# GpSimd adds the two halves of the products itself, in place of an accumulating transfer

## The chip, the cores and the metric

One Trainium2 chip, one of its cores. The metric is the device time of one execution, in microseconds (us). The engines are TensorE (PE; its weight loads are PEld), VectorE (DVE), ScalarE (ACT), GpSimd (POOL) and SyncE (SP, which here only issues transfers).

## What is computed

A recommendation tower over a batch of 1024: 39 embeddings of 16 numbers each are gathered, two layers of a compressed interaction network follow, and an MLP ends it.

```python
def cin_layer(x0, xk, W, b):                      # x0: (1024, 39, 16)
    out = jnp.einsum('bhd,bmd,shm->bsd', xk, x0, W) + b[None, :, None]
    return jax.nn.relu(out)

e = stack([tbl_f[ids[:, f]] for f in range(39)], axis=1)
x1 = cin_layer(e, e, W1, b1)                      # (1024, 128, 16)
x2 = cin_layer(e, x1, W2, b2)                     # (1024, 128, 16)
z = concatenate([x1.sum(-1), x2.sum(-1)], axis=-1)
h = concatenate([z, dense_ctx], axis=1)
h = maximum(h @ W_top1 + b_top1, 0)
h = maximum(h @ W_top2 + b_top2, 0)
y = h @ W_top3
```

The change touches only the second layer: for each batch row and each of the 16 embedding columns d, the sum over the 39 features m of `x0[b, m, d]` times a row of 128 numbers that TensorE has made from `x1` and `W2[:, :, m]`.

## The kernel before

The batch is cut into 8 **tiles** of 128 rows, and the 16 embedding columns of a tile into 4 **chunks** of 4. A chunk is 512 columns wide for the first layer. In the second layer each of its 4 embedding columns is a **column tile**, `ct` in the code, with the 128 batch rows on the partitions: 128 column tiles in all, 16 a batch tile.

*TensorE* (L526 on) works off one list. For each chunk it goes through 40 banks of PSUM, 10 a column tile; a bank has the products with four features (512 numbers), the tenth with three, and takes three matmuls each (L564; `w2h` and `w2l` are a weight split into two parts, `x1h` and `x1l` the same for the first layer's result). Five banks form a ring. Between the banks of one chunk stand the seven matmuls of the first layer for the next chunk (L548, at the places `CONTRACT_AT`), and, at bank 28, four transposes that lift the chunk after it from `emb_rep` into the PSUM tile `e_rep` (L537, called the lift here). In chunks 17 and 29 the matmuls of the MLP's two batches are put in too.

*ScalarE and VectorE* share the banks of a column tile. ScalarE takes banks 0, 2, 4, 6 and 8: for each of its 20 features it multiplies 128 numbers by the embedding's value and writes them to `prod` (L363), five banks of 512 in a row. `prod` has three buffers (`P_RING`). VectorE takes the other banks and adds its 19 features into `acc` as it scales them (L468, L470). Later VectorE merges both, once a chunk for the chunk before: L479 adds the two accumulators, L483 adds GpSimd's sum `a_sum`, L490 applies the ReLU and adds to `p2acc`. They stand at banks 22, 27 and 29 (`MERGE_AT`). L431 multiplies `e_rep` by the shifted copies of the embeddings, `z`, for the first layer.

*GpSimd* gathers the embeddings (L255, one indirect transfer for each of the 39 features of a tile) and adds up the 20 products of each column tile, 2560 numbers a row, to 128:

1. L266 (`add_by_transfer`): a transfer adds the upper half of `prod`, 1280 numbers, to the lower half, once ScalarE has written the column tile;
2. L284 (`add_quarters`): 640 + 640 into `tree`;
3. L291 (`add_inner`): 256 + 256;
4. L296 (`add_pair`): 128 + 128;
5. L305 (`add_last`): the 128 left over is added, and the result goes to `a_sum`.

These five steps of different column tiles are staggered: in the step for `ct`, GpSimd issues the transfer of `ct`, then the adds of `ct - 1` and `ct - 2`. Before them come two or three gathers for a later tile, until all are issued (`gathers_before`: all gathers of tile t stand ahead of column tile 16t - 7). The last column tile has its first step as a GpSimd add, L272 (`add_first`).

Three waits tie this together. ScalarE starts a column tile only when L284 has read the buffer of `prod` it will write (`sum3`). SyncE copies a tile's gathered embeddings to `emb_rep` (L207) when all 39 gathers have landed, and TensorE's first lift of that tile waits for the copy; it is in the place of column tile 16t - 6. VectorE's merge L483 waits for `a_sum`. SyncE also stores each lifted chunk (L216) and loads the shifted copies `z` (L224, nine transfers a chunk).

Of the kernel before, what the change touches and what calls it, by code (L numbers as in the profile page):

```python
# [9 lines left out]
ALU = mybir.AluOpType  # L10
# [5 lines left out]
S = 128  # L16
# [6 lines left out]
CTS = CHUNKS * DC  # L23
# [11 lines left out]
NA, NV = len(A_BANKS), len(V_BANKS)  # L35
# [39 lines left out]
def build(nc, dram, tables, out):  # L75
    with ExitStack() as ctx:
# [6 lines left out]
        def sem(name):  # L83
            return ctx.enter_context(nc.semaphore(name))
# [64 lines left out]
        p1_done = sem("p1_done")  # L149

        bank_ready, a_free, v_step = sem("bank_ready"), sem("a_free"), sem("v_step")
        in_sum = [sem(f"in_sum{r}") for r in range(2)]
        sum3, sum2, sum1, sum0 = sem("sum3"), sem("sum2"), sem("sum1"), sem("sum0")
        sum_first = sem("sum_first")
        merge_step, p2_done = sem("merge_step"), sem("p2_done")
# [3 lines left out]
        def wait(eng, s, value):  # L159
            if value > 0:  # L160
                eng.wait_ge(s, value)
# [3 lines left out]
        def gathers_before(ct):  # L165
            return min((TILES - 1) * M, -(-M * (ct + 7) // 16))

        def v_steps(ct, i):
            return ct * VM + V_BEFORE[i]
# [72 lines left out]
        @block.gpsimd  # L242
        def _(pool):
            def gather(n):
                tile, f = divmod(n, M)
                if f == 0 and tile == 0:
                    pool.wait_ge(in_idx0, 16)
                if f == 0 and tile == 1:
                    pool.wait_ge(in_idx, 16)
                if f == 0 and tile >= E_SLOTS:  # L250
                    last = (tile - E_SLOTS + 1) * CPT * DC
                    pool.wait_ge(v_step, v_steps(last, 0))
                    pool.wait_ge(a_free, last * NA)
                    pool.wait_ge(lifted, (tile - E_SLOTS + 1) * CPT)
                nc.gpsimd.indirect_dma_start(  # L255
                    out=emb[:, tile % E_SLOTS, f * D:(f + 1) * D], out_offset=None, in_=tables[f],
                    in_offset=bass.IndirectOffsetOnAxis(ap=idx[:, tile, f:f + 1], axis=0),
                ).then_inc(in_emb[tile % E_SLOTS], 16)

            def products(ct):  # L260
                return prod[:, ct % P_RING, :, :].rearrange("p a n -> p (a n)")

            def add_by_transfer(ct):
                pool.wait_ge(a_free, (ct + 1) * NA)
                half = 2 * NA * S
                nc.gpsimd.dma_start(products(ct)[:, 0:half], products(ct)[:, half:2 * half], accum_op=ALU.add  # L266
                                    ).then_inc(in_sum[ct % 2], 16)

            def add_first(ct):
                half = 2 * NA * S  # L270
                pool.wait_ge(a_free, (ct + 1) * NA)
                nc.gpsimd.tensor_tensor(products(ct)[:, 0:half], products(ct)[:, 0:half], products(ct)[:, half:2 * half],  # L272
                                        ALU.add).then_inc(sum_first, 1)

            def add_quarters(ct):
                n = NA * S
                if ct < CTS - 1:
                    pool.wait_ge(in_sum[ct % 2], 16 * (ct // 2 + 1))
                else:
                    pool.wait_ge(sum_first, 1)  # L280
                wait(pool, sum0, ct - 1)
                if ct == 0:
                    pool.wait_ge(w1_summed, 1)
                nc.gpsimd.tensor_tensor(tree[:, ct % 2, 0:n], products(ct)[:, 0:n], products(ct)[:, n:2 * n], ALU.add  # L284
                                        ).then_inc(sum3, 1)

            def add_inner(ct):
                pool.wait_ge(sum3, ct + 1)
                t = tree[:, ct % 2, :]
                n = NA // 2 * S  # L290
                nc.gpsimd.tensor_tensor(t[:, 0:n], t[:, 0:n], t[:, n:2 * n], ALU.add).then_inc(sum2, 1)  # L291

            def add_pair(ct):
                pool.wait_ge(sum2, ct + 1)
                t = tree[:, ct % 2, :]
                nc.gpsimd.tensor_tensor(t[:, 0:S], t[:, 0:S], t[:, S:2 * S], ALU.add).then_inc(sum1, 1)  # L296

            def add_last(ct):
                pool.wait_ge(sum1, ct + 1)
                c, j = divmod(ct, DC)  # L300
                if j == 0:
                    wait(pool, merge_step, 3 * (c - 1))
                t = tree[:, ct % 2, :]
                last = (NA - 1) * S if NA % 2 else 2 * S
                nc.gpsimd.tensor_tensor(a_sum[:, c % 2, j, :], t[:, 0:S], t[:, last:last + S], ALU.add).then_inc(sum0, 1)  # L305

            for n in range(M):
                gather(n)
            begun = M
            for ct in range(CTS):  # L310
                for n in range(begun, M + gathers_before(ct)):
                    gather(n)
                begun = max(begun, M + gathers_before(ct))
                if ct < CTS - 1:
                    add_by_transfer(ct)
                if ct:
                    add_quarters(ct - 1)
                if ct > 1:
                    add_pair(ct - 2)
                if ct:  # L320
                    add_inner(ct - 1)
                if ct > 1:
                    add_last(ct - 2)
            add_pair(CTS - 2)
            add_last(CTS - 2)
            add_first(CTS - 1)
            add_quarters(CTS - 1)
            add_inner(CTS - 1)
            add_pair(CTS - 1)
            add_last(CTS - 1)  # L330

# [344 lines left out]
```

## Time and profile before

| | |
|---|---|
| median of 3 runs | 1255.2 us (1251.39 to 1255.94) |
| the profiled execution | 1253.83 us |
| its span, first to last instruction | 1252.0 us |
| mean granted clock of TensorE | 0.989 of full |
| busy: PE, DVE, ACT, POOL | 92%, 74%, 64%, 68% of the span |
| GpSimd's adds of 640, 256, 128, 128 (L284, L291, L296, L305) | 239.3, 136.7, 111.3, 89.1 us |
| the transfer issues L266, the gathers L255 | 127 of 975 ns, 312 of 990 ns |
| software queue (gathers, accumulating transfers) | 85.81 MB, 36.9% of the 16 DMA engines' span |
| hardware queue (SyncE's transfers) | 67.92 MB, 22.0% |

"Busy" is the time in which an engine had an instruction under way. Records of one engine overlap: an add that is dispatched behind a transfer issue begins in the record before the issue ends. How long one operation holds the engine is better read from start to start, or from end to end, of neighbours with no wait between them. The span is one execution's; the median is over three.

### The profile page before, as it was taken

To read this page: it belongs to the slowest core of one execution; us is meant where nothing else is said; L and a number is where in the kernel's file an instruction comes from. 1 tells how busy PE (TensorE), PEld (TensorE's weight loads), DVE (VectorE), ACT (ScalarE), POOL (GpSimd) and SP (SyncE) were. 2 spreads that over 40 slices of the span, in tenths; PEclk is the share of its full clock that TensorE was granted. 3 is DMA by queue.
4 is the path that set the end of the run, shared out by engine and by line. 5 is a ranking of instruction groups with operands and counts; after the bars stand their busy time and mean duration, and the time that the engine had idled before them with its cause. 6 is when DMAs were issued, how large, how long until landed. Compare 5 with 4: busy or idle time off the path is not lost.

```text
span 1252.0 us, 17389 instructions
## 1 busy us (share of the span) xinstructions
PE 1155.7 (92%) x4556; PEld 849.7 (68%) x4556; DVE 928.8 (74%) x2846; ACT 796.9 (64%) x2702; POOL 848.6 (68%) x956
## 2 busy tenths in 40 slices
PE   0069999999999999999999999999999999999996
PEld 0037777777777777777776567777777776776775
DVE  2028878887878878788887468888887888774786
ACT  3026766667667766667666466777666666664683
POOL 7725777877787777787786467777777773442455
PEclk9989999999999999999999999999999999999997
DMA  5145666666765666677666267666665676642541
GB/s 163 41 103 106 125 148 130 142 129 134 172 123 119 123 151 125 128 142 151 145 140 121 44 138 156 136 119 124 144 125 124 137 158 133 139 100 62 119 92 35
DMA packets 66346, 154.85 MB, mean 124 GB/s; under 512 B 13219, under 2 KB 18981, under 8 KB 66246
## 3 DMA queue, kind: packets, MB, share of 16 engines
q0 software_dynamic: 28272, 85.81, 36.9%
q1 hardware_dynamic: 37974, 67.92, 22.0%
q8 instruction: 36, 0.59, 0.2%
q14 instruction: 64, 0.52, 0.2%
HBM read 58.59 MB, written 4.20 MB: 50 GB/s over the span
## 4 chain that ended last, share of the span: by engine, by line
POOL 43%; DMA 23%; issue 20%; PE 10%; another core or an unknown queue 2%; ACT 1%; SPq 1%; DVE 0%; POOLq 0%; ACTq 0%; DVEq 0%
DMA prod<-prod 19%; POOL emb L255 15%; POOL tree L284 11%; PE bank L564 7%; POOL tree L291 5%; POOL prod L266 5%; POOL tree L296 3%; POOL a_sum L305 3%; PE l_acc L548 2%; DMA z<-e_shifted 2%; DMA emb_rep<-emb 1%; DMA e_shifted<-e_t 1%; SPq L224 1%; ACT prod L363 0%
## 5 line engine op out<-in xcount | busy, mean ns | idle before, releaser
L363 ACT ACTIVATE prod<-bank,emb 128x128 f32<-128x128 f32 x2560 | 728.6, 372 | 368.8 <-PE bank L564 346.8
L470 DVE SCALAR_TENSOR_TENSOR acc<-bank,emb,acc 128x128 f32<-128x128 f32 x2176 | 613.3, 345 | 138.8 <-PE bank L564 118.4
L564 PE MATMUL bank<-w2h,x1h 128*128 128x512 f32 (+1 forms) x1280 | 537.0, 420 | 5.7 <-DVE x1l L436 4.5
L564 PE MATMUL bank<-w2l,x1h 128*128 128x512 f32 (+1 forms) x1280 | 499.7, 390 | 0.0
L564 PE MATMUL bank<-w2h,x1l 128*128 128x512 f32 (+1 forms) x1280 | 473.6, 433 | 0.0
L255 POOL DMA_INDIRECT emb<-tbl,idx x312 | 309.0, 990 | 82.0 <-issue 77.8
L564 PEld LDWEIGHTS bank<-w2h,x1h 128*128 128x128 f32 x1280 | 242.3, 189 | 119.2 <-issue 54.0
L564 PEld LDWEIGHTS bank<-w2h,x1l 128*128 128x128 f32 x1280 | 241.1, 188 | 87.5 <-issue 35.1
L266 POOL DMA_DIRECT2D prod<-prod x127 | 123.9, 975 | 243.7 <-ACT prod L363 239.7
L284 POOL TENSOR_TENSOR tree<-prod 128x640 f32<-128x640 f32 x128 | 239.3, 1870 | 66.5 <-DMA prod<-prod 66.4
L564 PEld LDWEIGHTS bank<-w2l,x1h 128*128 128x128 f32 x1280 | 241.8, 189 | 60.1 <-issue 17.5
L548 PE MATMUL l_acc<-z,w 117*128 117x512 f32 (+1 forms) x448 | 233.5, 604 | 16.1 <-DVE z L431 12.6
L431 DVE TENSOR_TENSOR z<-e_rep,z 117x512 f32<-117x512 f32 (+1 forms) x224 | 152.9, 684 | 121.0 <-DMA z<-e_shifted 80.3
L291 POOL TENSOR_TENSOR tree<-tree 128x256 f32<-128x256 f32 x128 | 136.7, 1068 | 0.2
L548 PEld LDWEIGHTS l_acc<-z,w 117*128 117x128 f32 (+1 forms) x448 | 84.3, 192 | 43.5 <-DVE z L431 16.7
L296 POOL TENSOR_TENSOR tree<-tree 128x128 f32<-128x128 f32 x128 | 111.3, 870 | 0.1
L305 POOL TENSOR_TENSOR a_sum<-tree 128x128 f32<-128x128 f32 x128 | 89.1, 696 | 0.2
L537 PE MATMUL e_rep<-ident_f,emb_rep 128*117 128x128 f32 x128 | 29.3, 352 | 63.6 <-DMA emb_rep<-emb 63.6
L537 PEld LDWEIGHTS e_rep<-ident_f,emb_rep 128*117 128x117 f32 x128 | 29.0, 287 | 67.7 <-issue 57.9
L470 DVE SCALAR_TENSOR_TENSOR acc<-bank,emb,b_row 128x128 f32<-128x128 f32 x128 | 44.8, 350 | 27.1 <-PE bank L564 25.0
L468 DVE TENSOR_SCALAR acc<-bank,emb 128x128 f32<-128x128 f32 x128 | 44.1, 344 | 0.0
L347 ACT COPY e_t<-e_rep 117x512 f32<-117x512 f32 x32 | 19.5, 611 | 34.7 <-PE e_rep L537 33.8
(75 smaller groups left out, 299.7 us busy)
## 6 DMA issues: line engine op xcount, KB each, us to landing
prod<-prod POOLq DMA_DIRECT2D x127, 640.0 KB
z<-e_shifted SPq DMA_DIRECT2D x160, 234.0 KB
emb_rep<-emb SPq DMA_DIRECT2D x8, 936.0 KB
z<-e_shifted SPq DMA_DIRECT2D x96, 78.0 KB
emb<-tbl,idx POOLq DMA_INDIRECT x312
z<-e_shifted SPq DMA_DIRECT2D x32, 156.0 KB
e_shifted<-e_t SPq DMA_DIRECT2D x32, 128.0 KB, 2.8
prod<-w_by_h SPq DMA_DIRECT2D x3, 832.0 KB
```

The costliest lines, as they stand in the source:

```text
L255: nc.gpsimd.indirect_dma_start(out=emb[:, tile % E_SLOTS, f * D:(f + 1) * D], out_offset=None, in_=tables[f], in_offset=bass.IndirectOffse ...
L266: nc.gpsimd.dma_start(products(ct)[:, 0:half], products(ct)[:, half:2 * half], accum_op=ALU.add).then_inc(in_sum[ct % 2], 16)
L284: nc.gpsimd.tensor_tensor(tree[:, ct % 2, 0:n], products(ct)[:, 0:n], products(ct)[:, n:2 * n], ALU.add).then_inc(sum3, 1)
L291: nc.gpsimd.tensor_tensor(t[:, 0:n], t[:, 0:n], t[:, n:2 * n], ALU.add).then_inc(sum2, 1)
L296: nc.gpsimd.tensor_tensor(t[:, 0:S], t[:, 0:S], t[:, S:2 * S], ALU.add).then_inc(sum1, 1)
L305: nc.gpsimd.tensor_tensor(a_sum[:, c % 2, j, :], t[:, 0:S], t[:, last:last + S], ALU.add).then_inc(sum0, 1)
L363: last = nc.scalar.activation(prod[:, ct % P_RING, i, n * S:(n + 1) * S], bank[:, (ct * NB + k) % RING, n * S:(n + 1) * S], ACT.Copy, scal ...
L431: nc.vector.tensor_tensor(z[0:rows, f % 2, t, :], e_rep[0:rows, :], z[0:rows, f % 2, t, :], ALU.mult).then_inc(f_made, 1)
L470: nc.vector.scalar_tensor_tensor(dst, src, scale, dst if step else b2_row[:, :], ALU.mult, ALU.add).then_inc(v_step, 1)
L537: last = nc.tensor.transpose(e_rep[0:KP * M, d * P:(d + 1) * P], by_d[:, q * DC + d, :], ident_f[:, :])
L548: nc.tensor.matmul(l1_acc[:, :], w1[0:rows, t, :], z[0:rows, f % 2, t, :], start=(t == 0), stop=(t == NF - 1)).then_inc(f_used, 1)
L564: last = nc.tensor.matmul(out_bank[:, 0:b - a], x, w[:, a:b], start=(n == 0), stop=(n == 2))
```

## The change

The transfer is gone. Each column tile has its 1280-element add on GpSimd (`add_first`, L265 of the new kernel), so `in_sum`, the semaphores of the transfers, go too, and `sum_first` counts the column tiles. The stagger becomes shorter: in the step for `ct` GpSimd does the first three adds of `ct` and, put between them, the last two of `ct - 1`.

```diff
@@ add_by_transfer, removed
-            def add_by_transfer(ct):
-                pool.wait_ge(a_free, (ct + 1) * NA)
-                half = 2 * NA * S
-                nc.gpsimd.dma_start(products(ct)[:, 0:half], products(ct)[:, half:2 * half], accum_op=ALU.add
-                                    ).then_inc(in_sum[ct % 2], 16)
-
             def add_first(ct):
                 half = 2 * NA * S
                 pool.wait_ge(a_free, (ct + 1) * NA)
@@ add_quarters
-                if ct < CTS - 1:
-                    pool.wait_ge(in_sum[ct % 2], 16 * (ct // 2 + 1))
-                else:
-                    pool.wait_ge(sum_first, 1)
+                pool.wait_ge(sum_first, ct + 1)
                 wait(pool, sum0, ct - 1)
@@ the loop over the column tiles, behind the gathers
-                if ct < CTS - 1:
-                    add_by_transfer(ct)
-                if ct:
-                    add_quarters(ct - 1)
-                if ct > 1:
-                    add_pair(ct - 2)
-                if ct:
-                    add_inner(ct - 1)
-                if ct > 1:
-                    add_last(ct - 2)
-            add_pair(CTS - 2)
-            add_last(CTS - 2)
-            add_first(CTS - 1)
-            add_quarters(CTS - 1)
-            add_inner(CTS - 1)
+                if ct == CTS - 1:
+                    add_pair(ct - 1)
+                    add_last(ct - 1)
+                add_first(ct)
+                if 0 < ct < CTS - 1:
+                    add_pair(ct - 1)
+                add_quarters(ct)
+                if 0 < ct < CTS - 1:
+                    add_last(ct - 1)
+                add_inner(ct)
             add_pair(CTS - 1)
             add_last(CTS - 1)
```

GpSimd's list in the stretch where gathers still run, one step with three gathers, before:

```order
L255 DMA emb<-tbl,idx 128x16 x3
L266 DMA prod<-prod 128x1280
L284 TENSOR_TENSOR tree<-prod 128x640
L296 TENSOR_TENSOR tree<-tree 128x128
L291 TENSOR_TENSOR tree<-tree 128x256
L305 TENSOR_TENSOR a_sum<-tree 128x128
L255 DMA emb<-tbl,idx 128x16 x2
```

And the same place in the changed kernel, whose lines are numbered anew:

```order
L254 DMA emb<-tbl,idx 128x16 x3
L265 TENSOR_TENSOR prod<-prod 128x1280
L286 TENSOR_TENSOR tree<-tree 128x128
L274 TENSOR_TENSOR tree<-prod 128x640
L295 TENSOR_TENSOR a_sum<-tree 128x128
L281 TENSOR_TENSOR tree<-tree 128x256
L254 DMA emb<-tbl,idx 128x16 x2
```

The wide add stands where the issue stood. The 640- and 256-element adds are now those of the column tile just written, the 128-element adds those of the one before it.

The end of GpSimd's list before, from the last transfer issue on:

```order
L266 DMA prod<-prod 128x1280
L284 TENSOR_TENSOR tree<-prod 128x640
L296 TENSOR_TENSOR tree<-tree 128x128
L291 TENSOR_TENSOR tree<-tree 128x256
L305 TENSOR_TENSOR a_sum<-tree 128x128
L284 TENSOR_TENSOR tree<-prod 128x640
L296 TENSOR_TENSOR tree<-tree 128x128
L291 TENSOR_TENSOR tree<-tree 128x256
L305 TENSOR_TENSOR a_sum<-tree 128x128
L296 TENSOR_TENSOR tree<-tree 128x128
L305 TENSOR_TENSOR a_sum<-tree 128x128
L272 TENSOR_TENSOR prod<-prod 128x1280
```

And in the changed kernel, from the wide add of the last column tile but one:

```order
L265 TENSOR_TENSOR prod<-prod 128x1280
L286 TENSOR_TENSOR tree<-tree 128x128
L274 TENSOR_TENSOR tree<-prod 128x640
L295 TENSOR_TENSOR a_sum<-tree 128x128
L281 TENSOR_TENSOR tree<-tree 128x256
L286 TENSOR_TENSOR tree<-tree 128x128
L295 TENSOR_TENSOR a_sum<-tree 128x128
L265 TENSOR_TENSOR prod<-prod 128x1280
```

Ahead of the last wide add there were the four adds behind the last transfer and two short ones; now there are the two short ones. What follows the last wide add is the same in both.

## Rows read from the trace of the kernel before

**Rows 1.** Busy time of each engine, its share of the span, instructions.
```profile
PE 1155.7 (92%) x4556; PEld 849.7 (68%) x4556; DVE 928.8 (74%) x2846; ACT 796.9 (64%) x2702; POOL 848.6 (68%) x956
```

**Rows 2.** PE's timeline, the lifts: start, us, what, [idle before <-releaser].
```profile
181.22 1.06 PE L537 MATMUL e_rep<-ident_f,emb_rep 128*117 128x128 f32 x4 [1.20 <-DMA emb_rep<-emb]
...
528.35 0.87 PE L537 MATMUL e_rep<-ident_f,emb_rep 128*117 128x128 f32 x4
...
562.31 0.87 PE L537 MATMUL e_rep<-ident_f,emb_rep 128*117 128x128 f32 x4
...
596.95 1.06 PE L537 MATMUL e_rep<-ident_f,emb_rep 128*117 128x128 f32 x4 [0.58 <-DMA emb_rep<-emb]
...
757.00 0.87 PE L537 MATMUL e_rep<-ident_f,emb_rep 128*117 128x128 f32 x4
...
1035.96 1.07 PE L537 MATMUL e_rep<-ident_f,emb_rep 128*117 128x128 f32 x4 [2.29 <-DMA emb_rep<-emb]
```

**Rows 3.** Waits from 181.2 to 597 us: total, times, longest.
```profile
POOL prod L266 <- ACT prod L363: 33.5, 15, 3.3
...
POOL tree L284 <- DMA prod<-prod: 32.5, 12, 3.4
DVE z L431 <- DMA z<-e_shifted: 30.9, 13, 3.4
```

**Rows 4.** POOL's timeline, one step with three gathers, one with two.
```profile
531.50 0.97 POOL L266 DMA_DIRECT2D prod<-prod  x1 [3.17 <-ACT prod L363]
...
539.33 1.02 POOL L266 DMA_DIRECT2D prod<-prod  x1
539.96 2.01 POOL L284 TENSOR_TENSOR tree<-prod 128x640 f32<-128x640 f32 x1
541.48 0.90 POOL L296 TENSOR_TENSOR tree<-tree 128x128 f32<-128x128 f32 x1
...
545.93 1.03 POOL L266 DMA_DIRECT2D prod<-prod  x1
```

**Rows 5.** The chain of waits: start, us, what.
```profile
52.96 4.31 DMA emb_rep<-emb
...
307.37 1.57 POOL tree L284
...
314.38 6.61 DMA emb_rep<-emb
```

**Rows 6.** The timeline at the end, POOL, DVE and ACT.
```profile
1224.51 0.68 DVE L483 TENSOR_TENSOR t_sum<-t_sum,a_sum 128x512 f32<-128x512 f32 x1
...
1225.79 1.89 POOL L284 TENSOR_TENSOR tree<-prod 128x640 f32<-128x640 f32 x1
1225.89 2.44 DVE L490 SCALAR_TENSOR_TENSOR p2acc<-t_sum,p2acc 128x512 f32<-128x512 f32 x1
...
1227.32 1.30 POOL L296 TENSOR_TENSOR tree<-tree 128x128 f32<-128x128 f32 x1
...
1231.81 1.14 ACT L363 ACTIVATE prod<-bank,emb 128x128 f32<-128x128 f32 x4 [0.26 <-PE bank L564]
...
1234.66 2.88 POOL L272 TENSOR_TENSOR prod<-prod 128x1280 f32<-128x1280 f32 x1
1234.80 3.15 DVE L483 TENSOR_TENSOR t_sum<-t_sum,a_sum 128x384 f32<-128x384 f32 x1 [0.95 <-POOL a_sum L305]
```

**Rows 7.** Waits from 94 to 175 us.
```profile
POOL prod L266 <- ACT prod L363: 33.9, 4, 20.4
...
POOL tree L284 <- DMA prod<-prod: 5.1, 2, 2.8
```

**Rows 8.** Waits from 1036 us to the end.
```profile
POOL prod L266 <- ACT prod L363: 108.5, 21, 10.9
```

**Rows 9.** Busy time by stretch, and the granted clock (PEclk), behind a lift.
```profile
core 0: us, PE busy (x) PEld busy (x) DVE busy (x) ACT busy (x) POOL busy (x), PEclk, DMA share, GB/s
1036.70:1041.00 4.30, 4.30 (x14) 3.64 (x14) 2.18 (x4) 2.52 (x9) 1.70 (x2) 0.60 0.09 19
```

More of the change, by code:

```diff
@@ L151, in build @@
         bank_ready, a_free, v_step = sem("bank_ready"), sem("a_free"), sem("v_step")
-        in_sum = [sem(f"in_sum{r}") for r in range(2)]
         sum3, sum2, sum1, sum0 = sem("sum3"), sem("sum2"), sem("sum1"), sem("sum0")
```

## The prediction

> **What bounds the kernel now.** I read the engines' busy time first, then TensorE's timeline for its period, then GpSimd's waits, then GpSimd's timeline for one step, and last VectorE beside GpSimd. TensorE is busy 92% of the span [rows 1], so it is the bound before the change. Its period is best read at the transposes that lift a chunk into `e_rep`, once a chunk of four column tiles. The undisturbed distance is 562.31 - 528.35 = 33.96 us [rows 2], so a batch tile (four chunks, 16 column tiles) needs at least 4 x 33.96 = 135.8 us of TensorE. The tiles' first lifts stand at 181.22, 596.95 (three tiles later), 757.00 and 1035.96 (two tiles later) [rows 2]: 138.6 us a tile, then 160.1 us for the tile in which the first MLP batch runs, then 139.5 us. About 3 us a tile are lost to small waits, and the queue of transfers has a hand in them: VectorE waits 30.9 us in three tiles for `z` [rows 3].
>
> The reader has to see next how near GpSimd is behind. In the three tiles from 181.2 to 597 it waits 33.5 us for products and 32.5 us for the accumulating transfer [rows 3], 66.0 in all, so **22.0 us a tile** is all the spare time it has. Then there is a tight loop that an engine table does not show. The last gather of a tile releases the copy into `emb_rep`, which releases the tile's first lift on TensorE; that lift already waits, 0.58 us at 596.95 and 2.29 us at 1035.96 [rows 2]. So GpSimd cannot fall behind without TensorE stopping at the next tile, whatever the three buffers of `prod` allow.
>
> **The change, part by part.**
>
> *The issue goes, the wide add comes.* One step of GpSimd before, with no wait in it: 539.33 - 531.50 = 7.83 us with three gathers, 545.93 - 539.33 = 6.60 us with two [rows 4]. From the start of the issue at 539.33 to the end of the 640-element add (539.96 + 2.01) are 2.64 us [rows 4]; that add without an issue ahead of it takes 1.57 [rows 5]; the issue is worth 1.07 us. The wide add is already in the kernel once, for the last column tile: 2.88 us [rows 6]. Upper bound: twice the 640-element add, 3.14. Lower bound: I have no row below 2.88, and the row is of the same shape, so I take it. Net **+1.81 us a step**. The order of the rest (an add of the column tile before between two dependent adds) keeps each dependent add one instruction apart, as before, so I cost its waits at nothing; if that cover failed, some 0.1 us a step would come on top.
>
> The GPSIMD Engine Reference of the Trainium skill (section 3.1) has 4497 ns for a float32 add of 2048 elements, which makes an estimate of 2.81 us for 1280. By it the forecast would be some 6 us lower; the measured 2.88 decides.
>
> *A tile of 16 steps.* 39 gathers in 16 steps are nine steps with two and seven with three: 9 x (6.60 + 1.81) + 7 x (7.83 + 1.81) = 143.2 us. The other way to it: 16 x 1.81 = 29.0 us are added to an engine that has 22.0 us to spare, so it overruns by 7 us before anything else is counted. At 143.2 us against TensorE's 135.8, **GpSimd becomes the bound** wherever gathers still run.
>
> *The port shared with VectorE.* Three merges a chunk on VectorE read two SBUF operands. The one that began at 1225.89, beside GpSimd's add from 1225.79, took 2.44 us, and the one at 1234.80 took 3.15 us, just until the 2.88 us add had ended and its own work was done [rows 6]; the same work took 0.68 at 1224.51, while GpSimd waited [rows 6]. GpSimd pays too: the 128-element add behind such a merge shows 1.30 us instead of 0.90 [rows 4, 6], about 0.5 us with what follows. So far most merges fall into gathers and waits of GpSimd. Afterwards GpSimd adds for 5.95 us of each 9, two thirds of the time: 12 merges a tile x 2/3 x 0.5 = 4.0 us. VectorE's own delay, up to 2.9 us a merge, costs nothing while GpSimd is the bound, since TensorE then has slack.
>
> The page SBUF — State Buffer of the Trainium skill (section "Who interferes with whom") states this as an exclusive lock for the whole instruction, between a VectorE instruction with two SBUF inputs and a GpSimd instruction that reads SBUF. By that rule the trace agrees (3.15 us behind 2.88), and it is the page's rule that speaks most against this change: where a transfer held no port of the engines, the longest GpSimd add of the step now holds it.
>
> *The loop.* The lift of a new tile comes late by what GpSimd is late, and then GpSimd waits once for the products of that delayed column tile: 0 to 2 us, taken as 1. A tile comes to 143.2 + 4.0 + 1.0 = **148.2 us**.
>
> *What the transfer gives back.* 1280 floats in each of 128 partitions, 640 KB a column tile, leave the queues. The copy to `emb_rep` takes 4.31 us on idle queues at 52.96 and 6.61 us under load at 314.38 [rows 5]; about 2 us once a tile, which only moves the loop's phase and is given to the first tile below. VectorE's waits for `z` shrink, but TensorE gains nothing by it while GpSimd holds the pace.
>
> *The sum, on the profiled span of 1252.0 us.*
> - To the first lift of tile 1: ten steps x 1.81 = 18 us against waits of 33.9 - 20.4 + 5.1 = 18.6 us [rows 7]. The copy is shorter, merges cost a little: +1.
> - Three tiles to 596.95: 3 x (148.2 - 138.6) = +28.8.
> - The tile with the MLP: TensorE needs 160.1, more than GpSimd's 148.2: 0.
> - Two tiles to 1035.96: 2 x (148.2 - 139.5) = +17.4, less 2 because the MLP stretch lets GpSimd catch up: +15.4.
> - After that no gathers are left: GpSimd waits 108.5 us for products there [rows 8], and 22 steps add 40. TensorE is the bound again: 0, as longer waits of VectorE at the port and shorter ones for `z` about cancel.
> - The end: the last wide add started at 1234.66 behind the last transfer's adds; ScalarE's products end at 1231.81 + 1.14 = 1232.95 [rows 6], and now only two short adds may stand between: -1.5.
>
> Together +43.7: span 1295.7, and with the 1.8 us around the span (1253.8 - 1252.0) **1297 us**. The profiled execution lies 1.4 below the median of 1255.2 us, within their scatter, so I leave the number there.
>
> **Rivals.**
> 1. *The port costs GpSimd little* (merges come at fixed places in TensorE's order and may keep falling into gathers, as most did). Tiles of 144.2 us: 5 x 4 = 20 less, 1277 us. Chance 0.17.
> 2. *The stops at each tile cost the clock too.* After the 2.29 us wait the granted clock is 0.60 from 1036.7 to 1041, between the 1.2 and the 2.4 GHz level [rows 9]: 4.3 x 0.4 = 1.7 us. If every lift now waits longer and this comes on top, and the wide add is nearer 3.0 than 2.88, I get 1309 us. Against it: behind the lift GpSimd, not TensorE, is late. Chance 0.13.
> 3. *Faster: the freed queues decide.* If the wide add took at most 2.1 us in the stream (2.88 - 12.4/16), GpSimd would need no more than TensorE's 135.8 a tile, and TensorE would lose its waits for transfers: 3 x 2.8 + 2 x 3.7 + 3 (MLP tile) + 1 + 1.5 = 21 less, 1232 us. For it: 30.9 us of waits for `z` in three tiles. Against it: the one row there is, 2.88. Chance 0.08.
> 4. *Level*: a wide add of about 2.4 us and few collisions, losses and gains cancelling, 1255 us. Chance 0.04.
> The forecast keeps 0.58.
>
> **Numbers.** Without the port, and with an add of 2.75 us instead of 2.88 (5 x 16 x 0.13 = 10 less), I come to 1266; with an add of 3.0 us and the clock to 1309 and some 7 more for an add up to the 3.14 bound on part of the steps; the range 1266 to 1316 leaves out the rivals 3 and 4 (0.12) and some tail. A measurement tells about 0.5% (6 us) from no change. Faster 0.08, same 0.05, slower 0.87.
>
> **What would show it.** Right: GpSimd's waits in the three middle tiles near 0 to 2 us a tile instead of 22; the tiles' first lifts 147 to 149 us apart and TensorE waiting several us at each for `emb_rep`, or for ScalarE, which waits for a buffer of `prod`; GpSimd's queue moving the gathers alone; merges of 1.5 to 3 us; after the last tile's lift the old pace. The wide add at 2.9 us and steps of 8.4 and 9.6 us check the price. Wrong: lifts less than 140 us apart, or GpSimd still waiting 10 us a tile for products.

## The result and the profile after

The changed kernel is **slower**: a median of 1292.9 us over five executions (1292.0 to 1300.7) against 1255.0 us before, a ratio of 1.033 with a 95% interval of 1.031 to 1.036. The forecast was 1297 us, slower. A second set of runs of the same kernel, at the end of the study, gave 1288.9 us (1288.3 to 1289.4), ratio 1.028 (1.024 to 1.032) to the kernel before, which had 1252.8 us in that set.

The profile shown here is of the longest of the first five executions, 1300.7 us with a span of 1298.9; the other four lie between 1292.0 and 1293.5. The last experiment has a second profile, of an execution of 1288.5 us; here they are called the first and the second profile.

First the page: busy time of each engine, and the software queue (packets, MB, share of the 16 DMA engines).

```profile
PE 1170.8 (90%) x4556; PEld 858.4 (66%) x4556; DVE 1005.6 (77%) x2846; ACT 797.7 (61%) x2702; POOL 1089.3 (84%) x956
...
q0 software_dynamic: 9984, 2.58, 2.4%
```

Against [rows 1], TensorE's busy share fell from 92% to 90% and GpSimd's rose from 68% to 84%. The software queue moves 2.58 MB instead of 85.81. TensorE's lifts, as in [rows 2] (start, us, what, idle before and what ended it):

```profile
184.45 1.06 PE L522 MATMUL e_rep<-ident_f,emb_rep 128*117 128x128 f32 x4 [4.23 <-DMA emb_rep<-emb]
...
629.17 1.21 PE L522 MATMUL e_rep<-ident_f,emb_rep 128*117 128x128 f32 x4 [3.75 <-DMA emb_rep<-emb]
...
796.15 0.87 PE L522 MATMUL e_rep<-ident_f,emb_rep 128*117 128x128 f32 x4
...
1087.76 1.21 PE L522 MATMUL e_rep<-ident_f,emb_rep 128*117 128x128 f32 x4 [3.69 <-DMA emb_rep<-emb]
```

Three tiles from 184.45 to 629.17 take 444.7 us, 148.2 each, against 138.6 before. The tile with the MLP takes 167.0 against 160.1, the two after it 291.6 against 279.0 together. Each of the lifts but the one behind the MLP waits 3.7 us or more for the copy, where the waits were 0.58 to 2.29. What waits in those three tiles (total, times, longest), to set beside [rows 3]:

```profile
PE e_rep L522 <- DMA emb_rep<-emb: 11.8, 3, 4.2
PE bank L549 <- DVE acc L455: 10.6, 12, 4.0
POOL prod L265 <- ACT prod L348: 8.1, 2, 4.5
```

GpSimd's 66 us of waits are down to 8.1. VectorE no longer waits for `z` at all in these tiles. But TensorE now waits for the banks that VectorE has to free (L549 is the matmul, L455 VectorE's scaled add): 10.6 us, up to 4.0 at once. GpSimd's step, against [rows 4]:

```profile
446.35 2.97 POOL L265 TENSOR_TENSOR prod<-prod 128x1280 f32<-128x1280 f32 x1
...
455.97 2.95 POOL L265 TENSOR_TENSOR prod<-prod 128x1280 f32<-128x1280 f32 x1
...
464.34 2.95 POOL L265 TENSOR_TENSOR prod<-prod 128x1280 f32<-128x1280 f32 x1
```

9.62 us with three gathers and 8.37 with two, where 9.64 and 8.41 were forecast.

The merges are the new thing (L464, L468 and L475 of the new kernel). The busy time of the instructions on `t_sum` over the length of three tiles, first before, then after; the two stretches begin at different places of the tile, but each holds 36 merges (stretch, its length, VectorE's busy us and count, TensorE's granted clock, DMA share, GB/s):

```profile
225.50:641.10 415.60, 27.91 (x36) 1.00 0.66 136
```

```profile
181.00:626.00 445.00, 63.94 (x36) 0.97 0.25 56
```

36 such instructions take 63.9 us instead of 27.9. The worst of them, in the timeline of the changed kernel:

```profile
483.02 2.97 POOL L265 TENSOR_TENSOR prod<-prod 128x1280 f32<-128x1280 f32 x1
...
483.27 6.26 DVE L475 SCALAR_TENSOR_TENSOR p2acc<-t_sum,p2acc 128x512 f32<-128x512 f32 x1
...
485.94 0.47 POOL L286 TENSOR_TENSOR tree<-tree 128x128 f32<-128x128 f32 x1
...
486.35 1.54 POOL L274 TENSOR_TENSOR tree<-prod 128x640 f32<-128x640 f32 x1
487.84 0.45 POOL L295 TENSOR_TENSOR a_sum<-tree 128x128 f32<-128x128 f32 x1
488.25 0.72 POOL L281 TENSOR_TENSOR tree<-tree 128x256 f32<-128x256 f32 x1
...
490.62 0.80 PE L549 MATMUL bank<-w2h,x1h 128*128 128x512 f32 x1 [3.95 <-DVE acc L455]
...
496.09 2.96 POOL L265 TENSOR_TENSOR prod<-prod 128x1280 f32<-128x1280 f32 x1 [4.49 <-ACT prod L348]
```

The merge began 0.25 us after the wide add and ended at 489.53. Its own work is 0.68 us, so it got its turn at 488.85, when all **five** adds of the step were about done, not when the wide add was. TensorE then stood 3.95 us for VectorE's bank, and GpSimd 4.49 us for the products of the column tile that came late by it.

### The profile page after: what moved, and what is told of

Read it like the earlier page. It is cut to its first block, busy times and chain, and to the rows that moved or that the text cites. A ratio compares the mean times of both kernels' runs of the same rounds, so it can differ in the third digit from the quotient of the medians.

```text
span 1298.9 us, 17389 instructions
## 1 busy us (share of the span) xinstructions
PE 1170.8 (90%) x4556; PEld 858.4 (66%) x4556; DVE 1005.6 (77%) x2846; ACT 797.7 (61%) x2702; POOL 1089.3 (84%) x956
## 3 DMA queue, kind: packets, MB, share of 16 engines
q0 software_dynamic: 9984, 2.58, 2.4%
## 4 chain that ended last, share of the span: by engine, by line
POOL 57%; PE 21%; issue 14%; DVE 2%; DMA 2%; another core or an unknown queue 2%; ACT 1%; SPq 0%; POOLq 0%; DVEq 0%; ACTq 0%
POOL prod L265 22%; PE bank L549 15%; POOL emb L254 13%; POOL tree L274 11%; POOL tree L281 5%; PE l_acc L533 4%; POOL a_sum L295 3%; POOL tree L286 3%; PE misc L568 1%; DVE acc L455 1%; DMA prod<-w_by_h 1%; DVE p2acc L475 1%; PE misc L571 1%; DMA z<-e_shifted 0%
## 5 line engine op out<-in xcount | busy, mean ns | idle before, releaser
L455 DVE SCALAR_TENSOR_TENSOR acc<-bank,emb,acc 128x128 f32<-128x128 f32 x2176 | 612.5, 342 | 177.8 <-PE bank L549 164.2
L549 PE MATMUL bank<-w2h,x1h 128*128 128x512 f32 (+1 forms) x1280 | 553.4, 432 | 24.7 <-DVE acc L455 20.2
L549 PE MATMUL bank<-w2l,x1h 128*128 128x512 f32 (+1 forms) x1280 | 504.3, 394 | 0.0
L265 POOL TENSOR_TENSOR prod<-prod 128x1280 f32<-128x1280 f32 x128 | 380.9, 2975 | 117.5 <-ACT prod L348 115.3
L549 PE MATMUL bank<-w2h,x1l 128*128 128x512 f32 (+1 forms) x1280 | 477.5, 437 | 0.0
L549 PEld LDWEIGHTS bank<-w2h,x1h 128*128 128x128 f32 x1280 | 246.0, 192 | 143.6 <-issue 66.0
L549 PEld LDWEIGHTS bank<-w2h,x1l 128*128 128x128 f32 x1280 | 244.6, 191 | 88.9 <-issue 35.1
L549 PEld LDWEIGHTS bank<-w2l,x1h 128*128 128x128 f32 x1280 | 245.5, 192 | 64.0 <-issue 22.9
L274 POOL TENSOR_TENSOR tree<-prod 128x640 f32<-128x640 f32 x128 | 200.0, 1562 | 0.2
L281 POOL TENSOR_TENSOR tree<-tree 128x256 f32<-128x256 f32 x128 | 94.0, 735 | 0.2
L286 POOL TENSOR_TENSOR tree<-tree 128x128 f32<-128x128 f32 x128 | 69.7, 544 | 0.2
L455 DVE SCALAR_TENSOR_TENSOR acc<-bank,emb,b_row 128x128 f32<-128x128 f32 x128 | 44.5, 347 | 29.4 <-PE bank L549 27.6
L295 POOL TENSOR_TENSOR a_sum<-tree 128x128 f32<-128x128 f32 x128 | 59.0, 461 | 0.2
L468 DVE TENSOR_TENSOR t_sum<-t_sum,a_sum 128x512 f32<-128x512 f32 (+2 forms) x33 | 57.1, 1730 | 0.5 <-POOL a_sum L295 0.5
L464 DVE TENSOR_TENSOR t_sum<-acc 128x512 f32<-128x512 f32 (+2 forms) x33 | 49.3, 1493 | 0.0
```

Source lines behind the costliest of these rows:

```text
L455: nc.vector.scalar_tensor_tensor(dst, src, scale, dst if step else b2_row[:, :], ALU.mult, ALU.add).then_inc(v_step, 1)
L549: last = nc.tensor.matmul(out_bank[:, 0:b - a], x, w[:, a:b], start=(n == 0), stop=(n == 2))
```

## The experiments

All but e4, e8, e10 and e12 are edits of the changed kernel; those four are edits of the kernel before.

**e1: two of three merges read one SBUF operand.** The merge sum goes to the PSUM tile `misc` wherever the MLP does not use it.

```diff
+                in_psum = c + 1 not in BATCH_IN and c < CHUNKS - 1
+                merged = misc[:, :].rearrange("p (j s) -> p j s", j=DC) if in_psum else t_sum
+                if n == 0 and in_psum and c in BATCH_IN:
+                    dve.wait_ge(mlp_act, MLP_STEPS * (BATCH_IN.index(c) + 1))
...
-                    nc.vector.tensor_tensor(t_sum[:, a:b, :], t_sum[:, a:b, :], a_sum[:, c % 2, a:b, :], ALU.add
+                    nc.vector.tensor_tensor(merged[:, a:b, :], merged[:, a:b, :], a_sum[:, c % 2, a:b, :], ALU.add
...
```

The first and the third merge have `merged` in place of `t_sum` too.

> The changed kernel with VectorE's merge sum t_sum in the PSUM tile misc (except in the two MLP chunks and the last one), so that two of the three merges of a chunk read one SBUF operand. Port theory: the merges of 2 to 6 us at the second and third place go back to 0.7 us, TensorE's stop of about 4 us behind each tile's first lift and GpSimd's wait of 4.5 us that follows it go, and GpSimd loses fewer half microseconds to VectorE: 1270 to 1282 us against 1293. Rival, GpSimd's own adds alone set the time and VectorE's waits lie beside them: 1290 to 1296.

Measured: 1273.5 us (1273.2 to 1274.9), ratio to the kernel before 1.015 (1.010 to 1.021); 19.4 less than the first set of the changed kernel and 15.4 less than the second. The second merge, where its sum is in PSUM (line, count, busy us, mean ns):

```profile
L472 DVE TENSOR_TENSOR misc<-misc,a_sum 128x512 f32<-128x512 f32 x29 | 20.0, 688 | 0.0
```

None of these 29 takes more than 0.69 us, nor does any third merge that reads `misc`. The first merge still reads two SBUF operands, and 6 of the 12 in three tiles still take over 1 us. Its lifts:

```profile
328.31 1.21 PE L526 MATMUL e_rep<-ident_f,emb_rep 128*117 128x128 f32 x4 [6.17 <-DMA emb_rep<-emb]
...
615.99 1.21 PE L526 MATMUL e_rep<-ident_f,emb_rep 128*117 128x128 f32 x4 [6.32 <-DMA emb_rep<-emb]
```

Two tiles of 143.8 us. The rival that VectorE's waits lie beside the path falls. In these tiles and the one ahead of them GpSimd stands idle for only 0.5 us before its wide adds, so 143.8 us a tile is close to its bare list of adds and gathers (143.2 forecast), and most of what lay above it came from the merges that now read one SBUF operand.

**e2: all gathers four column tiles earlier.**

```diff
-            return min((TILES - 1) * M, -(-M * (ct + 7) // 16))
+            return min((TILES - 1) * M, -(-M * (ct + 11) // 16))
```

> The changed kernel with every gather issued four column tiles earlier. Loop theory: the waits for emb_rep at the tiles' first lifts (3.8 us each) vanish, GpSimd no longer waits for products behind a lift, and the MLP tile loses its extra 7 us in part, but 143 us of work a tile remain: 1270 to 1284 us, GpSimd's wait for products near zero between 181 us and the last gather. Rival, throughput alone: GpSimd's list is as long as before, 1289 to 1296. A third: the late gathers are the whole loss, and the time falls to 1255 or below.

Measured: 1293.7 us (1293.1 to 1294.2), in the range of the rival. The lifts:

```profile
121.47 0.87 PE L522 MATMUL e_rep<-ident_f,emb_rep 128*117 128x128 f32 x4
...
333.77 0.87 PE L522 MATMUL e_rep<-ident_f,emb_rep 128*117 128x128 f32 x4
...
481.23 0.87 PE L522 MATMUL e_rep<-ident_f,emb_rep 128*117 128x128 f32 x4
...
628.72 0.87 PE L522 MATMUL e_rep<-ident_f,emb_rep 128*117 128x128 f32 x4
```

No lift waits any more, and these two tiles still take 147.5 us each; the one ahead of them takes 144.4 and the one behind the MLP 138.5. GpSimd never waits for products in the three tiles, but 35 of their 36 merges now take over 1 us, where the changed kernel has 15 of 36 in either profile. So 147.5 us is GpSimd's list with a collision at nearly every merge, and what the early gathers may have given, the collisions took. Why the merges now fall beside adds is not shown. Part of the result is something else: the third lift stands at 121.47 instead of 111.88, because three engines stood still at the start (ScalarE for 7.1 us, VectorE for 9.4):

```profile
92.11 0.58 ACT L332 COPY e_t<-e_rep 117x512 f32<-117x512 f32 x1 [7.11 <-remote]
...
95.65 3.20 ACT L348 ACTIVATE prod<-bank,emb 128x128 f32<-128x128 f32 x12 [2.95 <-remote]
95.70 0.35 DVE L455 SCALAR_TENSOR_TENSOR acc<-bank,emb,b_row 128x128 f32<-128x128 f32 x1 [9.38 <-remote]
```

What they waited for is in no record; it came with the longer run of gathers before the first column tile, in e12 and e13 too, and stays open.

**e3: a wide add of half the width**, 640 elements. It leaves out the other half of that add.

```diff
-                nc.gpsimd.tensor_tensor(products(ct)[:, 0:half], products(ct)[:, 0:half], products(ct)[:, half:2 * half],
+                nc.gpsimd.tensor_tensor(products(ct)[:, 0:640], products(ct)[:, 0:640], products(ct)[:, half:half + 640],
```

> The changed kernel with a wide add of 640 elements instead of 1280; it leaves out half of that add. If GpSimd's adds set the pace, a step is 1.4 us shorter, a tile needs some 125 us of GpSimd, TensorE is the bound again, and as the queues are free of the transfers it runs at nearly 136 us a tile: 1226 to 1240 us, below the kernel before. If something else in the change costs (the order of the adds, buffers that come free later), 1255 or more.

Measured: 1225.2 us (1224.2 to 1227.9).

```profile
315.56 0.87 PE L522 MATMUL e_rep<-ident_f,emb_rep 128*117 128x128 f32 x4
...
587.20 0.87 PE L522 MATMUL e_rep<-ident_f,emb_rep 128*117 128x128 f32 x4
```

Two tiles in 271.6 us, 135.8 each: TensorE's undisturbed period to the tenth, with none of the 3 us a tile lost before. So the change is worth 30 us of the 1255 where GpSimd can keep up, and its order and its buffers show no cost. How much of the 30 is the free queues' and how much the shorter stagger's, no run separates.

**e9: a wide add of 1024 elements**, the same edit with 1024, which leaves out a fifth of the add.

> The changed kernel with a wide add of 1024 elements; it leaves out a fifth of that add. By the rows 1280 elements take 2.96 us and 640 take 1.6, so a step is 0.55 us shorter and a tile 8.8: 139 us of GpSimd with the port's collisions, still a little over TensorE's 135.8: 1240 to 1256 us. Rival, GpSimd stops being the bound only at a much narrower add: over 1265.

Measured: 1238.8 us (1236.8 to 1240.4), a little under the range. The add (line, busy us, mean ns) and the effect:

```profile
L265 POOL TENSOR_TENSOR prod<-prod 128x1024 f32<-128x1024 f32 x128 | 310.6, 2426 | 120.4 <-ACT prod L348 117.7 <-issue 1.1
```

0.55 us less a step, and tiles of 137 to 139 us. Of the 54 us that e9 saves against the first set (50 against the second), 5 tiles x 16 x 0.55 = 44 are the shorter add: what the last 256 elements cost GpSimd is seen in the time. The rest is not assigned.

**e5: the wide adds in the order of the kernel before.**

```diff
...
                 add_first(ct)
-                if 0 < ct < CTS - 1:
-                    add_pair(ct - 1)
-                add_quarters(ct)
-                if 0 < ct < CTS - 1:
-                    add_last(ct - 1)
-                add_inner(ct)
+                if ct:
+                    add_quarters(ct - 1)
+                if ct > 1:
+                    add_pair(ct - 2)
+                if ct:
+                    add_inner(ct - 1)
+                if ct > 1:
+                    add_last(ct - 2)
...
```

> The changed kernel's wide adds in the order of the kernel before (the wide add where the transfer was issued, then the shorter adds of the two column tiles before it). Theory: the work decides, not the stagger: 1288 to 1300 us against 1293. Rival, the shorter stagger itself costs or gains: under 1285, or over 1303 because the buffers of prod come free one step later.

Measured: 1298.4 us (1297.7 to 1313.2), ratio to the kernel before 1.039 (1.032 to 1.046), which overlaps that of the first set. It is in the range of the theory that the work decides. The median is 5.5 us over the first set and 9.5 over the second, so the shorter stagger may be worth 5 us or so, which is not clear of the noise; `a_sum` comes later in the old order, and VectorE waits for it, which the changed kernel has once, for 0.5 us:

```profile
DVE t_sum L478 <- POOL a_sum L295: 40.0, 18, 3.7
```

**e14: the wide add as two adds of 640 elements in a row.**

```diff
+                for a in (0, half // 2):
+                    b = a + half // 2
+                    nc.gpsimd.tensor_tensor(products(ct)[:, a:b], products(ct)[:, a:b],
+                                            products(ct)[:, half + a:half + b], ALU.add).then_inc(sum_first, 1)
...
```

```profile
484.19 3.09 POOL L267 TENSOR_TENSOR prod<-prod 128x640 f32<-128x640 f32 x2
484.19 3.65 DVE L477 SCALAR_TENSOR_TENSOR p2acc<-t_sum,p2acc 128x512 f32<-128x512 f32 x1
...
487.25 0.91 POOL L288 TENSOR_TENSOR tree<-tree 128x128 f32<-128x128 f32 x1
```

The two halves run from 484.19 to 487.28, the merge has its turn at 487.16. The other five had their turn between the halves, as here, where the pair takes 3.53 us:

```profile
1089.81 3.53 POOL L267 TENSOR_TENSOR prod<-prod 128x640 f32<-128x640 f32 x2 [2.96 <-ACT prod L350]
...
1090.34 1.57 DVE L477 SCALAR_TENSOR_TENSOR p2acc<-t_sum,p2acc 128x512 f32<-128x512 f32 x1
```

Neither theory fits whole: the 6 us merges are gone, and the time did not fall. A pair that holds the merge off takes 3.09 us where the whole add takes 2.96, and a shorter instruction alone is no remedy.

**e13: e1 and e2 together.**

> The changed kernel with both e1 (merge sum in PSUM) and e2 (gathers four column tiles earlier). Theory: GpSimd's bare list is what is left, 143.5 us a tile as in e1, and the early gathers add nothing to that: 1266 to 1275 us. Rival, the two together release more, under 1262.

Measured: 1264.1 us (1262.8 to 1265.6), between the two ranges and 9 us under e1, though e2 alone gained nothing. So early gathers do gain once most collisions are gone. The first tile behind the start runs at TensorE's 135.8 us, the next two at 142.9 and 144.2, the MLP tile takes 165.5 (159.9 in e1), and the two behind it 135.8 and 138.3. I read this as a debt: GpSimd may fall behind by what the buffers of `prod` hold, once at the start and again behind the MLP, where it has caught up (it waits 7.7 us for products in the MLP tile). No run tests that reading by itself.

**e4: transfers up to column tile 105, adds from 106 on**, where no gathers are left.

```diff
...
+                if ct < FIRST_ADD:
+                    add_by_transfer(ct)
...
+                add_first(ct)
...
```

> The kernel before up to column tile 105, with transfers, and GpSimd's own wide adds only from column tile 106 on, where no gathers are left. The changed kernel's last stretch was 4.9 us shorter than that of the kernel before. Theory: GpSimd has room there, so this keeps the gain without the loss: 1247 to 1252 us against 1255. Rival: the port's collisions eat it, 1254 to 1258.

Measured: 1254.0 us (1248.5 to 1257.4), ratio 0.999 (0.997 to 1.002): no gain that can be told. My theory's 5 us do not show in the median. GpSimd had room (L273 is the add, L267 the transfer):

```profile
POOL prod L267 <- ACT prod L375: 126.8, 37, 19.4
...
POOL prod L273 <- ACT prod L375: 60.3, 19, 8.5
```

60.3 us of waits for products remain in the stretch with the adds, so it was not short of time. In this one profile the stretch from the last tile's first lift to the end is 210.5 us, 5.6 shorter than in the profile of the kernel before (216.1), and the tiles ahead of it, where the two kernels do the same, are together 5.0 us longer. e8, below, has transfers throughout and a last stretch of 211.6. So a single profile of that stretch does not tell 5 us, and whether the change shortens it stays open.

**e8: the kernel before with the merge sum in PSUM**, the edit of e1.

> The kernel before with the merge sum in PSUM as in e1. There GpSimd has 22 us a tile to spare and most merges fall into its gathers or waits: 1250 to 1255 us, no more than 0.4% faster. If the port matters without the change too, under 1248.

Measured: 1254.6 us (1250.0 to 1259.1), ratio 0.999 (0.996 to 1.001). The port costs nothing that can be measured without the change, and the 15 to 19 us of e1 belong to the change alone.

**e10: the transfer for even column tiles, GpSimd's add for odd ones**, in the old order.

```diff
...
-                if ct < CTS - 1:
-                    add_by_transfer(ct)
+                if ct % 2 == 0:
+                    add_by_transfer(ct)
+                elif ct < CTS - 1:
+                    add_first(ct)
```

What is left out counts the semaphores anew.

> The kernel before with GpSimd's own wide add for the odd column tiles and the transfer for the even ones. Theory: eight wide adds a tile are 8 x 1.9 = 15 us on GpSimd's 22 to spare, so TensorE stays the bound, and half of the transfers' traffic is gone: 1236 to 1248 us, faster than both kernels. Rival, any wide add in a stretch with gathers delays the next lift: 1256 to 1275.

Measured: **1238.9 us** (1237.3 to 1241.2), ratio to the kernel before 0.988 (0.984 to 0.992). It beats both kernels: 1.2% under the one before, 4.2% under the first set of the changed one. The queue, the lifts and the waits of the whole run, with one of the kernel before at the end:

```profile
q0 software_dynamic: 19200, 44.52, 20.3%
```

```profile
317.95 0.87 PE L539 MATMUL e_rep<-ident_f,emb_rep 128*117 128x128 f32 x4
...
454.51 0.87 PE L539 MATMUL e_rep<-ident_f,emb_rep 128*117 128x128 f32 x4
...
591.17 0.87 PE L539 MATMUL e_rep<-ident_f,emb_rep 128*117 128x128 f32 x4
```

```profile
POOL prod L266 <- ACT prod L365: 92.3, 36, 19.9
POOL prod L272 <- ACT prod L365: 85.0, 32, 10.0
DVE z L433 <- DMA z<-e_shifted: 78.2, 33, 3.7
...
PE l_acc L550 <- DVE z L433: 4.6, 8, 1.8
```

```profile
PE l_acc L548 <- DVE z L431: 12.6, 9, 6.9
```

Half of the transfers' traffic is gone, no lift waits, these two tiles take 136.6 us each (the others 136.7 to 138.0), and GpSimd still waits for products. VectorE's waits for `z` are hardly shorter than before (80.3 us there), but TensorE's own waits are: 4.6 us instead of 12.6 for `z` by way of VectorE, and nothing at the lifts of tiles 1 to 7, where the kernel before waits 6.1 us in all. Together these are 14 us, where the two spans differ by 15.3.

**e12: e10 with the merge sum in PSUM and gathers two column tiles earlier.**

> The mix of e10 (transfers for even column tiles, adds for odd ones) with the merge sum in PSUM and the gathers two column tiles earlier. e10 still loses 0.8 to 1.2 us a tile to small waits against the 135.8 of TensorE alone: 1230 to 1239 us. Rival, these waits are of the queues (VectorE for z) and stay: 1237 to 1241.

Measured: 1244.7 us (1243.0 to 1247.3), worse than e10 and outside both ranges. Its tiles are the same as those of e10 within 0.4 us (137.1, 136.6 and 136.9); 5 us are lost before the first of them, where the first lift of tile 1 stands at 185.51 instead of 180.52, as in e2.

**e15: the changed kernel again.**

> The changed kernel as it is, for a second profile: its first profiled execution was the longest of five (1300.7 us against 1292.0 to 1293.5 of the others). It held three merges of 6.2 us, each behind a tile's first lift, with a stop of TensorE of 4 us after each, and two tiles of 149.2 and 150.2 us. Theory: these are the extra 7 us, and an execution of 1293 us has tiles of 146 to 148 us and merges of at most 4.1 us. Rival: they belong to the kernel and are in every execution, and the 7 us lie elsewhere.

Measured: 1288.9 us (1288.3 to 1289.4). Its lifts, and two of its merges:

```profile
184.09 1.20 PE L522 MATMUL e_rep<-ident_f,emb_rep 128*117 128x128 f32 x4 [4.25 <-DMA emb_rep<-emb]
...
329.52 1.14 PE L522 MATMUL e_rep<-ident_f,emb_rep 128*117 128x128 f32 x4 [3.66 <-DMA emb_rep<-emb]
...
621.13 1.20 PE L522 MATMUL e_rep<-ident_f,emb_rep 128*117 128x128 f32 x4 [3.65 <-DMA emb_rep<-emb]
...
783.80 0.87 PE L522 MATMUL e_rep<-ident_f,emb_rep 128*117 128x128 f32 x4
...
1075.49 1.21 PE L522 MATMUL e_rep<-ident_f,emb_rep 128*117 128x128 f32 x4 [3.59 <-DMA emb_rep<-emb]
```

```profile
472.73 3.38 DVE L468 TENSOR_TENSOR t_sum<-t_sum,a_sum 128x512 f32<-128x512 f32 x1
...
479.62 3.39 DVE L475 SCALAR_TENSOR_TENSOR p2acc<-t_sum,p2acc 128x512 f32<-128x512 f32 x1
```

The three tiles take 145.4 to 145.8 us, and the merge behind the lift, 6.26 us in the first profile, takes 3.39: it had its turn when the wide add ended. No merge is longer than 4.1 us. The theory holds for this profile, and the three long merges do not belong to every execution. The 12.2 us between the two spans (1298.9 and 1286.7) are 7.7 us in the three tiles and 4.3 in the MLP tile; where each of the three long merges of the first profile stands, the second has one of 3.4 to 3.5. The executions of 1293 us of the first set have no profile, and what sets them 4 us above this set stays open; in this set the kernel before was 2.2 us shorter too.

## Why the prediction was right, step by step

- **The wide add.** Forecast 2.88 us, measured 2.96 in the stream; the issue it replaces was put a little too low at 1.07, and the step came out as forecast (8.37 and 9.62 us). e1 gives the nearly bare tile as 143.8 against 143.2.
- **GpSimd becomes the bound.** Right: e3 and e9 move the time with the width of the add, and the changed kernel's GpSimd waits 2.7 us a tile in the first profile, and not at all in the second, instead of 22.
- **The port.** Right in kind, wrong in form and size. I priced GpSimd's loss at 4.0 us a tile; by e1 and e15 collisions cost some 2 in all, in the first profile 1.5 to 6.4. What was wrong in the price is the share: I took two thirds of the merges, and 15 of 36 take over 1 us in the middle tiles. In e2, where 35 of 36 do and GpSimd does not wait, its tile is 3.7 us above e1's. The sentence that failed is that VectorE's delay "costs nothing while GpSimd is the bound", with 2.9 us as the longest. A merge that holds VectorE for 3 to 6 us stops TensorE, and GpSimd then waits for products that are late; and in the MLP tile and the last stretch, where TensorE is the bound, e1 is 2.8 and 2.7 us shorter than e15. In the whole, e1's 15.2 us against e15's span are 9.6 in the five tiles, 2.8 and 2.7.
- **The loop.** One us a tile, with 0 to 2 as bounds; GpSimd waited 8.1 us in three tiles of the first profile, 2.7 each, and not at all in those of the second. Loosened alone, in e2, it gains nothing, but with most collisions gone it is worth something: behind the first lift of tile 1, e13 is 14.9 us shorter than e1. So the prediction's sentence that GpSimd cannot fall behind in this kernel without TensorE stopping stands.
- **The terms of the sum**, first profile and, behind it, second: to the first lift +1 forecast, +3.2 and +2.9 measured; three tiles +28.8, measured +29.0 and +21.3; the MLP tile 0, measured +6.9 and +2.6; the two tiles after +15.4, measured +12.7 and +12.7; from there to the end -1.5, measured -4.9 and -4.8 (a difference that e4 and e8 put in doubt). The MLP tile is the term I missed: TensorE's 160 us exceed GpSimd's 148 only in sum. Before the MLP's matmuls begin, the chunk behind the lift is still late by GpSimd and the merges (42.0 and 37.4 us from lift to lift, 34.5 before, 35.3 in e1), and that time does not come back.
- **Where it was luck.** That the three tiles agree with the forecast to 0.2 us is chance: it is so only in the first profile, with its three long merges. The total came as near as it did because a price for the port and the loop that was too high, by 2.5 us a tile against the second profile (148.2 and 145.7), was met by the terms that I had too low, the first lift and the MLP tile.
- **The rivals.** Rival 1, few collisions, had tiles of 144.2 us; the second profile's 145.7 are nearer to it than to my 148.2, though the time of 1289 us is nearer to mine. Rival 3, at 0.08, had a condition that the kernel does not meet (an add of at most 2.1 us); e3, which meets it, runs at 1225 us, 7 below the 1232 I gave, and the last stretch holds more than that (205.1 us against 216.1, where I gave 1.5). Rival 4's wide add of 2.4 us is e9, which runs at 1239 us and not at 1255. Rival 2's add of nearly 3.0 us came true. Of its clock, the mean granted clock is 0.976 in the first profile and 0.980 in the second, against 0.989 before; in e2, without waits at the lifts, it is 0.991 and the time is no shorter, so no cost of the clock shows where GpSimd sets the pace.

## What to carry to other kernels

Before moving work from a transfer to an engine, take that engine's waits in one period of the loop and compare them with what is added: here 22 us against 29. If the sum is over, move the part that fits, as e10 does with half of the adds. An engine that runs adds without a gap also blocks the neighbour that shares its port, so its idle time was worth something.

## What the runs showed of the hardware that I had not expected

- A merge with two SBUF operands can wait for more than the GpSimd instruction under way. Of the 42 merges over 1 us in the first profile, 18 waited past at least two adds in a row, three of them through all five (5.6 us of waiting). In e14 the merge at 484.19 was not let in between two halves, and that at 1090.34 was. The Trainium skill, SBUF — State Buffer, section "Who interferes with whom", says that the second to issue blocks until the first finishes; the lock agrees with these traces, but what the waiter gets is not always the next turn. Nor does the one that begins first in the record always go first: the merge at 400.13, which takes 4.03 us, began 0.54 us ahead of the wide add at 400.67, during a gather, and waited for that add. What decides it, no run here shows.
- One SBUF operand is not always enough to stay out of it. The third merge of a tile's first chunk (L472) reads `t_sum` alone; in the first profile it takes 0.41 us in five of eight cases and 3.11 in the two that meet the wide add. Where its sum is in PSUM (e1) it takes 0.68 each time.
- The same kernel gave 1292.9 and 1288.9 us in two sets, each with a spread of 1 to 1.5 us but for one execution of 1300.7 in the first. Between the two profiles, 1300.7 and 1288.5 us, three merges differ by 3 us of waiting each: they begin 0.24 to 0.28 us behind the start of the wide add in one and 0.07 to 0.15 in the other. The place alone is not shown to be the reason: third merges that begin 0.35 and 0.53 us behind it had their turn at its end.
